# Three more blocks of the next layer's rows made ahead of a layer's last turn (graph layers, one core)

## Chip, cores and metric

One core of a Trainium2 chip (trn2). The metric is the device time of one execution in microseconds, the median of several runs. The profile is one execution on the chip, taken by the hardware profiler.

## What is computed

3125 nodes with 128 features, 103125 edges with one of 9 types. Three relational layers, then a residual and a layer norm, then an attention layer over the same edges with a second residual and norm. The change touches only the three relational layers:

```python
out = embeddings
for l in range(3):
    X = einsum('ne,ref->rnf', out, weights[l])          # 9 products for each node
    msg = X[edge_type, src] + biases[l][edge_type]      # one row for each edge
    hidden = segment_sum(msg, dest, num_segments=3125)  # added up by destination
    out = relu(hidden) if l + 1 < 3 else hidden
```

## The kernel before

**Rows of a layer.** The nodes are cut into 25 blocks of 128. For a block, TensorE multiplies the block (in `hB`) with the layer's nine weight matrices in three matmul groups (`make_x`, L1176), VectorE adds the bias and puts the three results into one of five slots of `xst` (`take_made`, L676, one add for each group, called a make below), and SyncE stores the slot to the layer's table in HBM (`store`, L901, one DMA of 576 KB).

**Tiles and steps.** The edges are sorted by destination and cut into 806 tiles of 128 edges. GpSimd gathers the 128 rows of a tile from the table with one indirect DMA (L1010) into one of 62 slots of `grow`. SyncE waits for each tile in order and passes it on (L907). The destinations are cut into 31 groups of 102 nodes. A layer is 840 steps in 35 turns of 24: a step multiplies a tile with a one-hot matrix of one group (TensorE L1132; VectorE makes the one-hot at L581 and adds the product to the group's sums `hn` at L652). A tile that crosses a group's border is used in two steps. Where a tile is used is data; by the end of a layer the step number runs some 30 ahead of the tile number. In the same turns 10 cells of a table of edge counts are multiplied (VectorE L586 and L587, five matmuls a cell at L1141), until all 840 cells are done, in turn 13 of the third layer. When a group's cells are complete, ScalarE copies and stores them (L1312 to L1325).

**Between layers.** A layer's table must be whole before the next layer's first gather, since any edge may point at any node. The sums of finished groups are turned (`turn_sums`, L1165), passed through relu to `hB` (`take_turned`, L662), and made into rows. Four early portions do this inside the layer: `AT_TURN` = turns 9, 16, 23 and 31 each begin with a portion of five blocks, on two PSUM banks (`PAIR_BANKS`). A portion stands in the program order of TensorE and VectorE ahead of its turn; it begins when all steps before it have been added, and the turn's steps come after it. SyncE issues the stores of a portion among the tiles it passes on (`STORE_AT`). After the layer's last step the late part follows on three banks: 6 groups are turned and blocks 20 to 24 made and stored. Then the again part turns the other 25 groups and makes blocks 0 to 19 a second time, whatever the data; its stores are conditional. They are done only where the edges were spread so unevenly that a portion ran before its groups were finished (`overrun`, `again_made`), which is tested once, when the groups' ends are known. Then the steps of the next layer begin.

**What GpSimd waits for.** Before the first gather of a layer it waits until the stores of all 25 blocks have landed (one semaphore for each slot of `xst`). After that a gather may not overwrite a slot that is in use: from tile 60 on, every fourth gather waits for a count of used steps (`s_used`): tile t waits until step t - 29 has been used. The first 60 gathers of a layer wait for nothing.

Of the kernel before, what the change touches and what calls it, by code (L numbers as in the profile page):

```python
# [22 lines left out]
I32 = mybir.dt.int32  # L23
I16 = mybir.dt.int16
ALU = mybir.AluOpType
# [3 lines left out]
P = 128  # L29
U = 8  # L30
HALF = 4
RB = 102
# [15 lines left out]
def gnn_program(nc, x, src, dst, edge_type, weights, biases, beta, out):  # L48
    N, D = x.shape
    E = src.shape[0]  # L50
    L, R = weights.shape[0], weights.shape[1]
    NB = -(-N // P)
# [14 lines left out]
    GT = -(-E // P)  # L67
# [31 lines left out]
    XU = 5  # L99
# [3 lines left out]
    XN = NB // XU  # L103
# [1 line left out]
    assert BANKS == 7  # L105
    WIDTH = [min(512, NP - 512 * c) for c in range(BANKS)]

    EARLY = NB // XU - 1
    BLOCKS = [range(XU * k, XU * k + XU) for k in range(EARLY)]
    LATE_BLOCKS = range(XU * EARLY, NB)  # L110
    REACH = [P * XU * (k + 1) // RB + 1 if P * XU * (k + 1) % RB else P * XU * (k + 1) // RB for k in range(EARLY)]
    GROUPS = [range(REACH[k - 1] if k else 0, REACH[k]) for k in range(EARLY)]
    CUT = P * XU * EARLY // RB
    LATE_GROUPS, AGAIN_GROUPS = range(CUT, MB), range(0, CUT)
    AGAIN_BLOCKS = range(0, XU * EARLY)
    AT_TURN = [-(-(REACH[k] * NT // MB + BODY) // BODY) for k in range(EARLY)]
    PAIR_BANKS, ALL_BANKS = (6, 7), (5, 6, 7)
    EARLY_STORES, ALL_STORES = EARLY + 1, 2 * EARLY + 1
    assert AT_TURN[-1] < TURNS and all(a < b for a, b in zip(AT_TURN, AT_TURN[1:]))
    STORE_AT = {}  # L120
    for k in range(EARLY):
        for j, b in enumerate(BLOCKS[k]):
            STORE_AT[AT_TURN[k] * BODY + 12 + 2 * j] = b
    assert len(STORE_AT) == len(AGAIN_BLOCKS) and max(STORE_AT) < GT

    CG = NB // JB
    CW = JB * RB
# [32 lines left out]
    with ExitStack() as ctx:  # L160
        def sb(name, shape, dt=F32):
            return ctx.enter_context(nc.sbuf_tensor(name, shape, dt))
# [33 lines left out]
        top = sb("top", [P, NB])  # L196
        rden = sb("rden", [P, NB])
        overrun = sb("overrun", [P, EARLY + 1])
        again_made = sb("again_made", [P, 2], I32)


        REGION = 26900
# [96 lines left out]
        s_xd = [sem(f"s_xd{u}") for u in range(XU)]  # L299
# [41 lines left out]
        def values_of(eng, a, k, most, n, least=0):  # L341

            return nc.values_load_multi_w_load_instructions(
                a[0:1, bass.ds(k * n, n)], engines=[eng.engine], min_val=least, max_val=most)[1]
# [22 lines left out]
        def reg_wait(eng, s, value):  # L367

            eng.wait_ge(s, value)
            eng.nop(nofuse=True)  # L370
# [3 lines left out]
        def _(dve):  # L374
# [15 lines left out]
            nc_ = dve  # L390
# [98 lines left out]
            for k in range(EARLY):  # L489
                ins = nc_.tensor_scalar(overrun[:, k:k + 1], te[:, REACH[k] - 1:REACH[k]], float(AT_TURN[k] * BODY), None, ALU.is_gt)  # L490
            step(ins)
            step(nc_.tensor_reduce(overrun[:, EARLY:EARLY + 1], overrun[:, 0:EARLY], AX.X, ALU.max))
            nc_.tensor_copy(again_made[:, 0:1], overrun[:, EARLY:EARLY + 1])
            nc_.tensor_scalar(again_made[:, 1:2], overrun[:, EARLY:EARLY + 1], float(16 * EARLY), None, ALU.mult)
            step(nc_.memset(ends[:, MB - 1:MB], CQ + 1), "ends")
            past_t = gix[:, 0:NT].bitcast(F32)
            step(nc_.tensor_scalar(past_t, iota_s, endcol[:, 0:1], None, ALU.is_ge), "past")
# [56 lines left out]
            for t in range(EP):  # L554
                k = t % KR
# [129 lines left out]
            for l in range(L):  # L685
                if l:
                    take_turned(LATE_GROUPS, ALL_BANKS)
                    take_made(l, LATE_BLOCKS, ALL_BANKS)
                    take_turned(AGAIN_GROUPS, ALL_BANKS)
# [3 lines left out]
                for i in range(0, TURNS):  # L693
                    if l < L - 1 and i in AT_TURN:
                        k = AT_TURN.index(i)
                        take_turned(GROUPS[k], PAIR_BANKS)
                        take_made(l + 1, BLOCKS[k], PAIR_BANKS)
                    take_tiles(l, i, i < full)
# [12 lines left out]
            for b in range(0, NB, 4):  # L711
                n = min(4, NB - b)
# [150 lines left out]
        def _(sp):  # L863
# [22 lines left out]
            for q in range(NB * XC):  # L886
                b, c = q // XC, q % XC
# [10 lines left out]
            def store(l, b, cond=None):  # L898
                given[0] += XC
                sp.wait_ge(s_xe, given[0])  # L900
                sp.dma_start(xv[l][b * P:(b + 1) * P, :, :],  # L901
                             xst[:, b % XU, :].rearrange("p (r d) -> p r d", r=R), cond=cond).then_inc(s_xd[b % XU], 16)

            def pass_on(l):
                for t in range(GT):
                    sp.wait_ge(s_g[t % GR], 16 * (ROUNDS * l + t // GR + 1))
                    sp.sem_inc(s_seq, 1)  # L907
                    if l < L - 1 and t in STORE_AT:
                        store(l + 1, STORE_AT[t])

            sp.wait_ge(s_d, marks["ends"])
            needed = values_of(sp, again_made, 0, 1, 1)[0]
            pass_on(0)
            for l in range(1, L):
                for b in LATE_BLOCKS:
                    store(l, b)
# [2 lines left out]
                pass_on(l)  # L919

            for u in range(XU):
                sp.wait_ge(s_xd[u], 16 * ALL_STORES * (L - 1))
            sp.wait_ge(s_cst, 32 * CG * MB)

            def load_absent(k):
# [26 lines left out]
            for i in range(XN):  # L952
                sp.wait_ge(s_res, i + 1)
                lo, hi = i * XU, min((i + 1) * XU, NB - 1)
# [6 lines left out]
        @block.gpsimd  # L961
        def _(pool):
            nc_ = pool
            nc_.memset(ident[:, :], 0.0).then_inc(s_pool, 1)
            nc_.memset(ltri, 1.0).then_inc(s_pool, 1)
            nc_.memset(ones[:, :], 1.0).then_inc(s_pool, 1)
            nc_.memset(diag[:, :], 0.0).then_inc(s_pool, 1)
            nc_.iota(iota_w[:, :], pattern=[[1, RB]], base=0, channel_multiplier=0,
                     allow_small_or_imprecise_dtypes=True).then_inc(s_pool, 1)
            nc_.iota(iota_s, pattern=[[1, NT]], base=0, channel_multiplier=0,  # L970
                     allow_small_or_imprecise_dtypes=True).then_inc(s_pool, 1)
            nc_.iota(steps_down[:, :].rearrange("p (b m) -> p b m", m=P), pattern=[[P, CG], [0, P]], base=0, channel_multiplier=1,
                     allow_small_or_imprecise_dtypes=True).then_inc(s_pool, 1)
            nc_.iota(number[:, :], pattern=[[P, TC]], base=0, channel_multiplier=1,
                     allow_small_or_imprecise_dtypes=True).then_inc(s_pool, 1)
            pool.wait_ge(s_pool, 8)
            nc_.affine_select(out=ident[:, :], in_=ident[:, :], compare_op=ALU.not_equal, fill=1.0, base=0,
                              pattern=[[-1, P]], channel_multiplier=1).then_inc(s_pool, 1)

            nc_.affine_select(out=ltri, in_=ltri, compare_op=ALU.is_gt, fill=0.0, base=0,  # L980
                              pattern=[[1, P]], channel_multiplier=-1).then_inc(s_pool, 1)
            pool.wait_ge(s_pool, 10)

            nc_.tensor_scalar(negi[:, :], ident[:, :], -1.0, None, ALU.mult).then_inc(s_pool, 1)
            nc_.tensor_copy(diag[:, P:2 * P], ident[:, :]).then_inc(s_pool, 1)
            pool.wait_ge(s_pool, 12)
            pool.sem_inc(s_pool, 1)

            pool.wait_ge(s_fill, 16)
            pool.wait_ge(s_d, marks["cells"])  # L990
            for t in range(CP):
                pool.indirect_dma_start(  # L992
                    out=table, out_offset=bass.IndirectOffsetOnAxis(ap=pay[:, t, 1:2], axis=0),
                    in_=pay[:, t, 0:1], in_offset=None).then_inc(s_scat, 16)

            pool.wait_ge(s_d, marks["rows"])
            again = values_of(pool, again_made, 1, 16 * EARLY, 1)[0]
            for l in range(L):
                if l == 0:
                    for u in range(X0):  # L1000
                        pool.wait_ge(s_x0d[u], 16 * (-(-(NB * XC - u) // X0)))
                else:
                    for u in range(XU):
                        reg_wait(pool, s_xd[u], again + 16 * (ALL_STORES * (l - 1) + EARLY_STORES))

                for t in range(GT):
                    last = t + SLOTS - 1 - GR + LAP
                    if t % SLOTS == 0 and t + SLOTS - 1 >= GR:
                        pool.wait_ge(s_used, NT // SLOTS * l + last // SLOTS + 1)
                    pool.indirect_dma_start(  # L1010
                        out=grow[:, t % GR * D:(t % GR + 1) * D], out_offset=None, in_=xts[l],
                        in_offset=bass.IndirectOffsetOnAxis(ap=gix[:, t:t + 1], axis=0),
                    ).then_inc(s_g[t % GR], 16)
# [3 lines left out]
        def _(pe):  # L1017
# [163 lines left out]
            for l in range(L):  # L1181
                if l:
                    turn_sums(LATE_GROUPS, ALL_BANKS, NT * l)
                    make_x(l, LATE_BLOCKS, ALL_BANKS)
                    turn_sums(AGAIN_GROUPS, ALL_BANKS, NT * l)
# [4 lines left out]
                for i in range(0, TURNS):  # L1190
                    if l < L - 1 and i in AT_TURN:
                        k = AT_TURN.index(i)
                        turn_sums(GROUPS[k], PAIR_BANKS, NT * l + i * BODY)
                        make_x(l + 1, BLOCKS[k], PAIR_BANKS)
                        pe.wait_ge(s_xe, made[0])
# [188 lines left out]
```

## Time and profile before

| what | value |
|---|---|
| median of 3 runs | 4012.15 us (4010.5 to 4013.2) |
| the profiled execution | 4012.3 us, its span 4010.6 us |
| TensorE (matmul) busy | 2913.1 us, 73% of the span |
| VectorE busy | 2799.0 us, 70% |
| GpSimd busy | 2586.7 us, 64% |
| ScalarE busy | 820.7 us, 20% |
| gathers from the tables of layers 1 and 2 | 1612, mean 945 ns |

A busy share is an average over stages with different limits. The stage that the change touches is short: the end of the first and of the second layer, and the first turns after it. It is read from the timeline there and from what each engine waited for. Times in rows count from the span's start; what stands in brackets at a row's end is the engine's idle time before it and what ended it.

### The profile page before, as it was taken

The numbers are of one execution on the slowest core, as the hardware profiler recorded it, in microseconds if no ns is written. First come the engines' busy times: TensorE is split into PE (matmuls) and PEld (weight loads), VectorE is DVE, ScalarE is ACT, GpSimd is POOL, SyncE is SP. The second block draws the span as 40 slices with busy tenths as digits, with TensorE's granted clock in tenths as the row PEclk, the third lists the DMA queues.
The fourth block names the chain that finished last, engine by engine and source line by source line (L and its number), as shares of the span: only waits on it lengthen the run. The fifth ranks groups of instructions, "written<-read, shape, count | busy, mean of one in ns | idle before, by whom it ended". The sixth has DMA issues, their size and how long they took to land.

```text
span 4010.6 us, 57296 instructions
## 1 busy us (share of the span) xinstructions
PE 2913.1 (73%) x14367; PEld 1879.1 (47%) x14369; DVE 2799.0 (70%) x9282; ACT 820.7 (20%) x1995; POOL 2586.7 (64%) x2738
## 2 busy tenths in 40 slices
PE   7799967677777678777777776787674444447998
PEld 4455544444444445444444443554443333335776
DVE  9988876676667667776767665878664333337999
ACT  2588810100110010100100010001100000004665
POOL 0677757777777775777777777567777777770000
PEclk9899988888889889998889888999885555557999
DMA  4100013443444343343344434333333221223664
GB/s 157 54 2 2 2 36 73 82 110 76 102 89 107 73 102 88 74 90 102 79 107 83 102 81 85 103 81 78 86 79 73 53 54 53 53 53 116 191 189 136
DMA packets 373882, 336.44 MB, mean 84 GB/s; under 512 B 262034, under 2 KB 326090, under 8 KB 373448
## 3 DMA queue, kind: packets, MB, share of 16 engines
q0 software_dynamic: 87104, 158.80, 18.8%
q1 hardware_dynamic: 83112, 113.25, 8.5%
q10 hardware_dynamic: 203360, 60.73, 6.3%
q8 instruction: 141, 2.31, 0.2%
q14 instruction: 165, 1.35, 0.1%
HBM read 225.44 MB, written 130.73 MB: 89 GB/s over the span
## 4 chain that ended last, share of the span: by engine, by line
POOL 43%; PE 24%; issue 16%; DVE 12%; DMA 3%; ACT 2%; DVEq 0%; SPq 0%; POOLq 0%; ACTq 0%
POOL region L1010 43%; PE ps L1087 9%; PE ps L1132 4%; PE ps L1141 3%; PE ps L1215 3%; DMA region<-x_of_type_in_layer,arrays 2%; PE ps L1243 2%; DVE region L652 2%; PE ps L1176 2%; DVE region L586 1%; DVE region L419 1%; DVE region L587 1%; DVE region L779 1%; DVE arrays L453 1%; DVE arrays L464 1%
## 5 line engine op out<-in xcount | busy, mean ns | idle before, releaser
L1010 POOL DMA_INDIRECT region<-x_of_type_in_layer,arrays x1612 | 1522.7, 945 | 552.0 <-issue 475.1
L1132 PE MATMUL ps<-region,oh 128*102 x5040 | 1115.0, 325 | 781.7 <-SPq L907 514.8
L1132 PEld LDWEIGHTS ps<-region,oh 128*102 128x102 f32 x5040 | 922.3, 204 | 1337.1 <-issue 1078.0
L1141 PE MATMUL ps<-region 128*128 128x510 f16 x4200 | 1358.8, 411 | 180.2 <-ACT ps L1301 136.2
L581 DVE TENSOR_SCALAR oh<-iota_w,arrays 128x102 f32<-128x102 f32 x2528 | 727.0, 289 | 1046.5 <-PE ps L1132 1022.7
L1010 POOL DMA_INDIRECT region<-x_of_type,arrays x806 | 763.7, 947 | 273.2 <-issue 272.0
L652 DVE TENSOR_TENSOR region<-region,ps 102x128 f32 x2520 | 714.9, 284 | 3.9 <-issue 3.9
L1141 PEld LDWEIGHTS ps<-region 128*128 128x128 f16 x4200 | 434.6, 104 | 247.6 <-issue 195.1
L1312 ACT COPY region<-ps 128x510 f32<-128x510 f32 x155 | 89.8, 579 | 2244.7 <-PE ps L1141 2244.2
L586 DVE TENSOR_SCALAR region<-ps,arrays 128x640 f16<-128x640 f16 x844 | 460.1, 545 | 0.0
L992 POOL DMA_INDIRECT scattered_edges<-region x304 | 296.2, 974 | 208.7 <-DVE shiftcol L483 110.4
L587 DVE TENSOR_SCALAR region<-ps,arrays 128x510 f16<-128x510 f16 x844 | 400.5, 475 | 0.0
L1087 PE MATMUL ps<-region 128*128 128x420 f16 x2016 | 362.4, 341 | 23.7 <-ACT region L1282 23.7
L1282 ACT ACTIVATE region<-region 128x128 f16<-128x128 f16 x1008 | 310.3, 389 | 71.0 <-DVE region L559 70.7
L1087 PEld LDWEIGHTS ps<-region 128*128 128x128 f16 x2016 | 195.8, 97 | 190.7 <-ACT region L1282 24.8
L560 DVE TENSOR_SCALAR region<-region 128x840 f16<-128x840 f16 x504 | 262.0, 520 | 0.0
L1176 PE MATMUL ps<-wsb,hB 128*128 128x384 f32 x540 | 212.4, 548 | 8.8 <-DVE hB L662 8.4
L676 DVE TENSOR_TENSOR region<-ps,bias 128x384 f32<-128x384 f32 x270 | 148.9, 552 | 66.4 <-PE ps L1176 63.0
L1243 PEld LDWEIGHTS ps<-nodes,region 128*128 128x128 f32 (+1 forms) x1250 | 163.9, 191 | 53.8 <-DVE region L779 28.5
L1243 PE MATMUL ps<-nodes,region 128*128 128x129 f32 (+1 forms) x1250 | 181.3, 282 | 7.2 <-DVE region L779 7.0
L1215 PE MATMUL ps<-hB,region 128*128 128x384 f32 (+1 forms) x450 | 170.9, 461 | 0.0
L1176 PEld LDWEIGHTS ps<-wsb,hB 128*128 128x128 f32 x540 | 104.8, 208 | 112.0 <-DVE region L676 53.0
(222 smaller groups left out, 1671.7 us busy)
## 6 DMA issues: line engine op xcount, KB each, us to landing
x_of_type_in_layer<-region SPq DMA_DIRECT2D x90, 576.0 KB
edge_counts<-region ACTq DMA_DIRECT2D x155, 255.0 KB
arrays<-edge_counts SPq DMA_DIRECT2D x40, 960.0 KB, 5.1
region<-x_of_type_in_layer,arrays POOLq DMA_INDIRECT x1612, 2.6
edge_absent<-region ACTq DMA_DIRECT2D x155, 127.5 KB
region<-edge_absent SPq DMA_DIRECT2D x40, 480.0 KB, 4.3
region<-x_of_type,arrays POOLq DMA_INDIRECT x806, 2.6
x_of_type<-x0st SPq DMA_DIRECT2D x51, 192.0 KB, 1.8
```

Source lines behind the costliest of these rows:

```text
L581: ins = nc_.tensor_scalar(oh[:, t % U, 0:RB], iota_r, rowf[:, t % NT:t % NT + 1], None, ALU.is_equal)
L586: nc_.tensor_scalar(cl[:, q % CR, :], lane_h, key1[:, q:q + 1], None, ALU.is_equal)
L587: nc_.tensor_scalar(cr[:, q % CR, :], lane_h[:, 0:CW], key2[:, q:q + 1], None, ALU.is_equal).then_inc(s_co, 1)
L652: nc_.tensor_tensor(h, h, ps[0:RB, 6 + n % 2, t * D:(t + 1) * D], ALU.add).then_inc(s_add, 1)
L992: pool.indirect_dma_start(out=table, out_offset=bass.IndirectOffsetOnAxis(ap=pay[:, t, 1:2], axis=0), in_=pay[:, t, 0:1], in_offset=None). ...
L1010: pool.indirect_dma_start(out=grow[:, t % GR * D:(t % GR + 1) * D], out_offset=None, in_=xts[l], in_offset=bass.IndirectOffsetOnAxis(ap=gi ...
L1087: mm = pe.matmul(ps[:, 2 * d + n, 0:HW], oh_q[:, k, d, :], oh_s[:, k, n * HW:(n + 1) * HW], start=False, stop=False, skip_group_check=True)
L1132: mm = pe.matmul(ps[0:RB, 6 + n % 2, t * D:(t + 1) * D], oh[:, u % U, 0:RB], grow[:, bass.ds(at[u % PAIRS], D)], start=True, stop=True)
L1141: mm = pe.matmul(ps[:, c, 0:CW], cl[:, q % CR, c * P:(c + 1) * P], cr[:, q % CR, :], start=False, stop=False, skip_group_check=True)
L1176: pe.matmul(ps[:, banks[j % len(banks)], 0:G3], hB[:, b * P:(b + 1) * P], wsb[:, l * R + 3 * c:l * R + 3 * c + 3, :].rearrange("p r d -> p ...
L1243: mm = pe.matmul(ps[0:w, 4 + c % 2, t * VW:(t + 1) * VW], ring[:, b % RING, t * P:t * P + w], nodes[:, j, :], start=False, stop=(j == NB - ...
L1282: ins = act.activation(oh_q[:, k, d, :], hot_q[:, k, :], ACT.Copy, scale=cols[:, 4 * t + 2 + d:4 * t + 3 + d])
```

## The change

The list of portions is now given by the blocks at which they end: 5, 10, 15, 20 and 23. A fifth portion, with blocks 20, 21 and 22 (nine makes) and three groups to turn (26 to 28), stands ahead of turn 34, the last of a layer. The late part turns three groups (28 to 30) and makes blocks 23 and 24; the again part turns 28 groups and makes 23 blocks. The stores of blocks 20 to 22 would fall after tile 805, so SyncE issues them once all tiles of the layer are passed on. Since blocks 23 and 24 use slots 3 and 4, the slots now have different numbers of conditional stores, and GpSimd reads two numbers for its waits instead of one. The test of the groups' ends covers the fifth portion too, with one more compare.

```diff
-    EARLY = NB // XU - 1
-    BLOCKS = [range(XU * k, XU * k + XU) for k in range(EARLY)]
-    LATE_BLOCKS = range(XU * EARLY, NB)
-    REACH = [P * XU * (k + 1) // RB + 1 if P * XU * (k + 1) % RB else P * XU * (k + 1) // RB for k in range(EARLY)]
+    ENDS_AT = list(range(XU, NB, XU)) + [NB - 2]
+    EARLY = len(ENDS_AT)
+    BLOCKS = [range(lo, hi) for lo, hi in zip([0] + ENDS_AT, ENDS_AT)]
+    LATE_BLOCKS = range(ENDS_AT[-1], NB)
+    REACH = [-(-P * b // RB) for b in ENDS_AT]
     GROUPS = [range(REACH[k - 1] if k else 0, REACH[k]) for k in range(EARLY)]
-    CUT = P * XU * EARLY // RB
+    CUT = P * ENDS_AT[-1] // RB
     LATE_GROUPS, AGAIN_GROUPS = range(CUT, MB), range(0, CUT)
-    AGAIN_BLOCKS = range(0, XU * EARLY)
+    AGAIN_BLOCKS = range(0, ENDS_AT[-1])
     AT_TURN = [-(-(REACH[k] * NT // MB + BODY) // BODY) for k in range(EARLY)]
-    EARLY_STORES, ALL_STORES = EARLY + 1, 2 * EARLY + 1
+    FIRST_STORES = XN
+    AGAIN_STORES = [sum(b % XU == u for b in AGAIN_BLOCKS) for u in range(XU)]
...
+            nc_.tensor_scalar(again_made[:, 1:2], overrun[:, EARLY:EARLY + 1], float(16 * (XN - 1)), None, ALU.mult)
+            nc_.tensor_scalar(again_made[:, 2:3], overrun[:, EARLY:EARLY + 1], float(16 * XN), None, ALU.mult)
...
                     if l < L - 1 and t in STORE_AT:
                         store(l + 1, STORE_AT[t])
+                for t in sorted(STORE_AT) if l < L - 1 else ():
+                    if t >= GT:
+                        store(l + 1, STORE_AT[t])
...
-            again = values_of(pool, again_made, 1, 16 * EARLY, 1)[0]
+            again = [values_of(pool, again_made, n, 16 * XN, 1)[0] for n in (1, 2)]
...
-                        reg_wait(pool, s_xd[u], again + 16 * (ALL_STORES * (l - 1) + EARLY_STORES))
+                        reg_wait(pool, s_xd[u], again[AGAIN_STORES[u] - XN + 1] + 16 * (FIRST_STORES * l + AGAIN_STORES[u] * (l - 1)))
```

## Rows read from the trace of the kernel before

**Rows 1.** What GpSimd waited for: total us, times, longest us.

```profile
POOL region L1010 <- DMA x_of_type_in_layer<-region: 58.3, 2, 29.4
POOL region L1010 <- PE ps L1132: 19.8, 55, 2.4
```

**Rows 2.** Timeline of GpSimd: start us, us, what, [idle before, what ended it].

```profile
1575.74 0.94 POOL L1010 DMA_INDIRECT region<-x_of_type_in_layer,arrays  x1 [28.90 <-DMA x_of_type_in_layer<-region]
...
1652.79 0.94 POOL L1010 DMA_INDIRECT region<-x_of_type_in_layer,arrays  x1 [2.40 <-PE ps L1132]
...
2613.85 0.94 POOL L1010 DMA_INDIRECT region<-x_of_type_in_layer,arrays  x1 [29.43 <-DMA x_of_type_in_layer<-region]
...
2689.70 0.94 POOL L1010 DMA_INDIRECT region<-x_of_type_in_layer,arrays  x1 [1.24 <-PE ps L1132]
```

**Rows 3.** Busy us (instructions): stretch, length, PE, PEld, DVE, ACT, POOL, PEclk, DMA, GB/s.

```profile
1575.74:1652.79 77.05, 65.55 (x256) 39.62 (x256) 56.91 (x160) 8.11 (x13) 56.66 (x60) 0.93 0.28 69
```

**Rows 4.** Timeline of VectorE at the end of layer 0: last add, makes.

```profile
1556.91 0.29 DVE L652 TENSOR_TENSOR region<-region,ps 102x128 f32 x1
...
1560.86 0.56 DVE L676 TENSOR_TENSOR region<-ps,bias 128x384 f32<-128x384 f32 x1 [1.81 <-PE ps L1176]
...
1566.50 1.78 DVE L676 TENSOR_TENSOR region<-ps,bias 128x384 f32<-128x384 f32 x3 [0.16 <-PE ps L1176]
...
1570.37 1.78 DVE L676 TENSOR_TENSOR region<-ps,bias 128x384 f32<-128x384 f32 x3 [0.16 <-PE ps L1176]
```

**Rows 5.** Timeline of VectorE, two blocks of the again part after layer 0.

```profile
1577.15 1.13 DVE L676 TENSOR_TENSOR region<-ps,bias 128x384 f32<-128x384 f32 x2 [1.07 <-PE ps L1176]
...
1579.09 1.13 DVE L676 TENSOR_TENSOR region<-ps,bias 128x384 f32<-128x384 f32 x2 [0.16 <-PE ps L1176]
```

**Rows 6.** Timeline of VectorE, layer 0: fourth portion and turn 31 after it.

```profile
1444.34 0.29 DVE L652 TENSOR_TENSOR region<-region,ps 102x128 f32 x1
...
1448.45 0.56 DVE L676 TENSOR_TENSOR region<-ps,bias 128x384 f32<-128x384 f32 x1 [1.81 <-PE ps L1176]
...
1455.88 0.56 DVE L676 TENSOR_TENSOR region<-ps,bias 128x384 f32<-128x384 f32 x1 [0.15 <-PE ps L1176]
...
1460.65 0.56 DVE L676 TENSOR_TENSOR region<-ps,bias 128x384 f32<-128x384 f32 x1 [0.16 <-PE ps L1176]
...
1468.82 0.28 DVE L652 TENSOR_TENSOR region<-region,ps 102x128 f32 x1
...
1486.62 0.29 DVE L652 TENSOR_TENSOR region<-region,ps 102x128 f32 x1
```

**Rows 7.** Busy us and granted clock, TensorE in two stretches of that portion.

```profile
1446.60:1451.50 4.90, 4.80 (x8) 2.42 (x8) 1.72 (x4) 0.00 (x0) 3.68 (x5) 0.50 0.53 86
1451.50:1461.30 9.80, 9.01 (x24) 3.42 (x22) 6.70 (x12) 0.00 (x0) 7.36 (x9) 1.00 0.43 79
```

**Rows 8.** Timeline of VectorE, the adds around the dearest and cheapest portion.

```profile
1010.22 0.29 DVE L652 TENSOR_TENSOR region<-region,ps 102x128 f32 x1
...
1035.88 0.28 DVE L652 TENSOR_TENSOR region<-region,ps 102x128 f32 x1
...
2048.03 0.29 DVE L652 TENSOR_TENSOR region<-region,ps 102x128 f32 x1
...
2071.35 0.28 DVE L652 TENSOR_TENSOR region<-region,ps 102x128 f32 x1
```

**Rows 9.** Timeline of VectorE: last adds of turns 33 and 34.

```profile
1534.21 0.29 DVE L652 TENSOR_TENSOR region<-region,ps 102x128 f32 x1
...
2575.13 0.29 DVE L652 TENSOR_TENSOR region<-region,ps 102x128 f32 x1
...
2595.79 0.29 DVE L652 TENSOR_TENSOR region<-region,ps 102x128 f32 x1
```

**Rows 10.** Timeline of ScalarE, layer 2: the 29th of 31 groups of counts.

```profile
2889.40 2.42 ACT L1318 ACTIVATE region<-region,big 128x2550 bf16<-128x2550 f32 x1
```

**Rows 11.** Busy us (instructions) of the cells' matmuls (L1141) after that.

```profile
2889.40:3100.00 210.60, 83.37 (x245) 26.38 (x245) 0.74 0.39 81
```

More of the change, by code:

```diff
@@ L106, in gnn_program @@
     WIDTH = [min(512, NP - 512 * c) for c in range(BANKS)]
-    EARLY = NB // XU - 1
-    BLOCKS = [range(XU * k, XU * k + XU) for k in range(EARLY)]
-    LATE_BLOCKS = range(XU * EARLY, NB)
-    REACH = [P * XU * (k + 1) // RB + 1 if P * XU * (k + 1) % RB else P * XU * (k + 1) // RB for k in range(EARLY)]
+    ENDS_AT = list(range(XU, NB, XU)) + [NB - 2]
[3 more added lines that the diff above has]
+    REACH = [-(-P * b // RB) for b in ENDS_AT]
     GROUPS = [range(REACH[k - 1] if k else 0, REACH[k]) for k in range(EARLY)]
-    CUT = P * XU * EARLY // RB
+    CUT = P * ENDS_AT[-1] // RB
     LATE_GROUPS, AGAIN_GROUPS = range(CUT, MB), range(0, CUT)
-    AGAIN_BLOCKS = range(0, XU * EARLY)
+    AGAIN_BLOCKS = range(0, ENDS_AT[-1])
     AT_TURN = [-(-(REACH[k] * NT // MB + BODY) // BODY) for k in range(EARLY)]
     PAIR_BANKS, ALL_BANKS = (6, 7), (5, 6, 7)
-    EARLY_STORES, ALL_STORES = EARLY + 1, 2 * EARLY + 1
+    FIRST_STORES = XN
+    AGAIN_STORES = [sum(b % XU == u for b in AGAIN_BLOCKS) for u in range(XU)]
+    assert NB == XU * XN and set(AGAIN_STORES) <= {XN - 1, XN}
     assert AT_TURN[-1] < TURNS and all(a < b for a, b in zip(AT_TURN, AT_TURN[1:]))
@@ L123, in gnn_program @@
             STORE_AT[AT_TURN[k] * BODY + 12 + 2 * j] = b
-    assert len(STORE_AT) == len(AGAIN_BLOCKS) and max(STORE_AT) < GT
+    assert sorted(STORE_AT.values()) == list(AGAIN_BLOCKS)
     CG = NB // JB
@@ L198, in gnn_program @@
         overrun = sb("overrun", [P, EARLY + 1])
-        again_made = sb("again_made", [P, 2], I32)
+        again_made = sb("again_made", [P, 3], I32)
         REGION = 26900
@@ L493, in _ @@
             nc_.tensor_copy(again_made[:, 0:1], overrun[:, EARLY:EARLY + 1])
-            nc_.tensor_scalar(again_made[:, 1:2], overrun[:, EARLY:EARLY + 1], float(16 * EARLY), None, ALU.mult)
+            nc_.tensor_scalar(again_made[:, 1:2], overrun[:, EARLY:EARLY + 1], float(16 * (XN - 1)), None, ALU.mult)
+            nc_.tensor_scalar(again_made[:, 2:3], overrun[:, EARLY:EARLY + 1], float(16 * XN), None, ALU.mult)
             step(nc_.memset(ends[:, MB - 1:MB], CQ + 1), "ends")
@@ L921, in _ @@
             for u in range(XU):
-                sp.wait_ge(s_xd[u], 16 * ALL_STORES * (L - 1))
+                sp.wait_ge(s_xd[u], 16 * (FIRST_STORES + AGAIN_STORES[u]) * (L - 1))
             sp.wait_ge(s_cst, 32 * CG * MB)
```

## Prediction

> **What bounds the kernel now.** I read the waits of GpSimd first, then its timeline at the two layer borders, then what VectorE and TensorE do around them. In the waits, the gathers of layers 1 and 2 lose 58.3 us to two waits for the stored rows, one at each border, and 19.8 us in 55 pieces to TensorE [rows 1]. The timeline says where: GpSimd stands still for 28.90 and 29.43 us before the first gather of layers 1 and 2 [rows 2]. That gap is what the change shortens. The next row of the same timeline matters more: after 60 gathers that wait for nothing [rows 3], the gather of tile 60 is held by TensorE for 2.40 us in layer 1 and 1.24 us in layer 2 [rows 2]. The 60 gathers take 75 us, and the hold lasts until step 31 of the new layer has been used. So at both borders two chains run side by side: GpSimd's (stores, then 60 gathers) and the consumer's, meaning TensorE and VectorE (late part, again part, 32 steps). The consumer's is the longer one, by about 2 and 1 us. From tile 60 on GpSimd sets the pace, so the time at which tile 60 goes out carries through to the layer's end. What moves the total is the moment at which step 31 is used, not the moment of the first gather.
>
> **The late part gets shorter.** At full clock a block costs 1.935 us there (from 1566.50 to 1570.37 for two blocks [rows 4]); three blocks less are 5.8 us. Turning three groups less saves a little: from the last add to the first make it is 3.66 us with six groups (1557.20 to 1560.86 [rows 4]) and 3.82 us with seven (1444.63 to 1448.45 [rows 6]), so 0.16 us a group and 0.5 us for three. Stores leave as each block is made, so the last one leaves 6.3 us sooner after the last add.
>
> **The again part gets longer by the same.** It makes three blocks and turns three groups more. A block costs 1.94 us (1577.15 to 1579.09 [rows 5]): +5.8 and +0.5 us. From a layer's last add to its successor's step 31 the consumer has the same work as before, since late and again part together always make 25 blocks. For it the change at the border is 0.
>
> **The fifth portion is new work.** It isn't moved work: its three blocks are made again behind the border. Its nearest row is the fourth portion in layer 0. There VectorE's last add ends at 1444.63 and its next one begins at 1468.82: 24.19 us without a step [rows 6]. Of this, 3.82 us pass before the first make, 12.76 us are 15 makes, and 7.61 us pass from the last make (ends 1461.21) to the next add. The new portion has nine makes: makes 10 to 15 took 4.77 us (from the end of the ninth, 1456.44, to 1461.21). It has four groups less to turn: 0.6 us. That leaves 24.19 - 4.77 - 0.64 = 18.8 us. The eight portions of before lie between 23.03 us (2048.32 to 2071.35) and 25.37 us (1010.51 to 1035.88) [rows 8], which gives 17.6 to 20.0 us.
>
> The restart is part of this price: TensorE ran at half its clock (0.50, 1.2 GHz) for the first 4.9 us of the fourth portion's makes, 8 matmuls in 4.80 us, and at 1.00 (2.4 GHz) for the next 24 in 9.01 us [rows 7]. The Trainium skill, TensorE: Matmul & The Clock Gate, Part 1, says that the throttled state is the default and activity releases it, which speaks against cutting work into one more portion. By a portion that began at full clock the price would be about 1.8 us less (8 matmuls at 0.375 instead of 0.60 us); the trace shows the half clock, and the sum keeps it.
>
> **What hides it.** Only waiting that the consumer already does in turn 34. After a portion tiles are plentiful and 24 steps run at VectorE's own pace: 18.1 us from first add to last (1468.82 to 1486.91 [rows 6]). I take this for the new turn 34; all its tiles will have landed by then, since GpSimd's last gather goes out 28.9 us before 1575.74 [rows 2]. So from the last add of turn 33 to the last add of the layer: 18.8 + 18.1 = 36.9 us. Before it was 1534.50 to 1557.20 = 22.7 us in layer 0 (with [rows 4]) and 2575.42 to 2596.08 = 20.7 us in layer 1 [rows 9]. The layer's last add moves by +14.2 and +16.2 us.
>
> **Sum.** GpSimd's first gather moves by 14.2 - 6.3 = +7.9 us at the first border and by 16.2 - 6.3 = +9.9 us at the second, against its own earlier pace: even the gap that was to shrink grows, to about 36.8 and 39.3 us. Tile 60 waits for the consumer and moves by +14.2 and +16.2 us, so its hold grows by 6.3 us each, to about 8.7 and 7.5 us. Both shifts reach the end, since GpSimd paces layer 1 after tile 60 and all of layer 2: 14.2 + 16.2 = 30.4 us. On the profiled execution's 4012.3 us (span 4010.6) that is 4042.7; the median of the runs is 0.15 us lower, so 4042.5 us.
>
> **Edits taken as nothing.** One more compare and one more product on single columns of VectorE in the setup: an add of 102x128 takes 0.29 us [rows 4], so at most 0.6 us; below nothing it can't be. One register load more on GpSimd lies ahead of the first gathers, where it waits anyway, and is under the same bound. SyncE: the three stores come behind the last tile it passes on, so no tile waits behind them; by then their makes are done (portion from 1534.50, 3.2 us and 8.0 us of makes, so about 1546), and they land long before the two late stores. If that cover failed, a store would be late by no more than the two behind it, some 4 us of GpSimd's chain, which has 6.3 us of slack against the consumer's. The portion's slots 0 to 2 of xst hold blocks whose stores went out among tiles 756 to 760, some 30 tiles before the portion.
>
> **Rivals.** (a) *The portion costs nothing.* If the consumer waited for tiles in turn 34 for the portion's whole length, only the border would count: the first gather comes 6.3 us earlier, and tile 60 is held 6.3 us longer. 4012, no change. For it: TensorE does wait for tiles over much of the program. Against it: the slack in turn 34 is 22.7 and 20.7 us less 18.1, under 5 and 3 us, against 18.8.
>
> (b) *The gain that the change reaches for, faster.* Hidden portion, and tile 60 not held: GpSimd is the pace, and it starts 6.3 us earlier twice, 4012.15 - 12.6 = 3999.6. It decides if GpSimd's chain is the longer one; the rows show the hold by TensorE at both borders before the change [rows 2], so it needs two things to be wrong at once. The busy times over those 77 us can't decide it: VectorE 56.91, GpSimd 56.66 us [rows 3]. The Trainium skill, Perfetto Trace Analysis, Optimization Strategy, has one look for the gaps of the most-contended engine and make what they wait for come sooner; with GpSimd taken for it, that rule leads to this rival, and the 2.40 and 1.24 us holds behind the gap are what it would overlook.
>
> (c) *The portion costs what I say, but tile 60 isn't held.* Only GpSimd's start counts: 7.9 + 9.9 = 17.8 us, 4030. It needs the consumer to be some 6 us faster behind the border than before; nothing in the rows offers that.
>
> (d) *Dearer.* A group's counts come to be copied within turn 34 or the hold grows into later tiles: a few us at each border, 4050 or more.
>
> (e) *It doesn't do what it says.* If group 28 ended after step 816, where turn 34 begins, all blocks would be stored a second time and GpSimd would wait for 23 blocks of 1.94 us at each border, some 45 us on top of the shift of its first gather (7.9 and 9.9 us), about 4120. The counts of the 29th group are complete at 2889.40 [rows 10], and 245 matmuls, five a cell, come after [rows 11]: it ends at cell 840 - 49 = 791, below 816. Excluded but for an error of mine.
>
> **How the numbers follow.** Forecast 0.78, (a) 0.06, (b) 0.04, (c) 0.07, (d) 0.04, (e) 0.01. The forecast's own range: portions of 17.6 to 20.0 us give 28.0 to 32.8 us, and with 1 us a border for the turn's pace and the small edits 4039 to 4047. To hold 8 in 10 the range reaches to (c) and the near part of (d): 4029 to 4050. A measurement of this kernel tells 0.2% (8 us) from no change: slower 0.78 + 0.07 + 0.04 + 0.01 = 0.90, same 0.06, faster 0.04.
>
> **What would show it.** Right: between the last add of turn 33 and the first of turn 34 some 19 us without a step in layers 0 and 1; GpSimd's gaps at the borders near 37 and 39 us; tile 60 held for about 8 us; layer 2 shifted as a whole by 30 us. Wrong: an unchanged last add (the portion is hidden), tile 60 not held (GpSimd sets the border), or a second pass of stores that lengthens the gap to 70 us or more.

## The result

| | kernel before | changed kernel |
|---|---|---|
| median, measured side by side (6 runs each) | 4012.56 us | 4040.49 us |
| profiled execution, its span | 4012.3 us, 4010.6 us | 4039.88 us, 4038.1 us |
| ratio, 95% interval | | 1.0071 (1.0058 to 1.0083) |

The changed kernel is slower by 28 us, 0.7%; forecast were 4042.5 us and slower. Nearly all of it is at the two layer borders. First GpSimd's timeline in the changed kernel, the rows that answer to [rows 2] (start us, us, what, idle before and what ended it):

```profile
1580.40 0.94 POOL L1017 DMA_INDIRECT region<-x_of_type_in_layer,arrays  x1 [33.10 <-DMA x_of_type_in_layer<-region]
...
1663.47 0.94 POOL L1017 DMA_INDIRECT region<-x_of_type_in_layer,arrays  x1 [8.44 <-PE ps L1139]
...
2636.23 0.94 POOL L1017 DMA_INDIRECT region<-x_of_type_in_layer,arrays  x1 [41.34 <-DMA x_of_type_in_layer<-region]
...
2717.15 0.94 POOL L1017 DMA_INDIRECT region<-x_of_type_in_layer,arrays  x1 [6.31 <-PE ps L1139]
```

The gap that the change was to shorten has grown at both borders, from 28.90 and 29.43 to 33.10 and 41.34 us. The hold of tile 60 has grown too, from 2.40 and 1.24 to 8.44 and 6.31 us. Tile 60 goes out 10.7 us later in layer 1 (1652.79 to 1663.47) and 27.5 us later in layer 2 (2689.70 to 2717.15). After that nothing is added: the spans differ by 27.5 us. In total, by the waits of GpSimd (us, times, longest), against [rows 1]:

```profile
POOL region L1017 <- DMA x_of_type_in_layer<-region: 74.4, 2, 41.3
POOL region L1017 <- PE ps L1139: 30.6, 54, 8.4
```

16.1 us more for the stored rows and 10.8 us more for TensorE make 26.9 of the 27.5 us. The cause stands ahead of the border, in VectorE's timeline around the fifth portion in layer 0 (last add before it, first and last make, first add after it) and then at the layer's end, answering to [rows 6] and [rows 4]:

```profile
1532.36 0.29 DVE L656 TENSOR_TENSOR region<-region,ps 102x128 f32 x1
...
1535.52 0.56 DVE L680 TENSOR_TENSOR region<-ps,bias 128x384 f32<-128x384 f32 x1 [1.81 <-PE ps L1183]
...
1542.44 0.56 DVE L680 TENSOR_TENSOR region<-ps,bias 128x384 f32<-128x384 f32 x1 [0.36 <-PE ps L1183]
...
1549.41 0.28 DVE L656 TENSOR_TENSOR region<-region,ps 102x128 f32 x1
...
1567.83 0.29 DVE L656 TENSOR_TENSOR region<-region,ps 102x128 f32 x1
...
1575.03 1.78 DVE L680 TENSOR_TENSOR region<-ps,bias 128x384 f32<-128x384 f32 x3 [0.71 <-PE ps L1183]
```

From 1532.65 to 1549.41 no step is added: 16.8 us. The layer's last add ends at 1568.12 instead of 1557.20. The late part then ends at 1576.81, and the first gather comes 12.3 us after the last add (1568.12 to 1580.40) where it came 18.5 us after it before (1557.20 to 1575.74). So the late part did get 6.3 us shorter, as the change intends. At the second border 17.8 us became 10.8 (2596.08 to 2613.85 before, 2625.39 to 2636.23 now).

In layer 1 the portion was longer:

```profile
2584.99 0.29 DVE L656 TENSOR_TENSOR region<-region,ps 102x128 f32 x1
...
2607.30 0.28 DVE L656 TENSOR_TENSOR region<-region,ps 102x128 f32 x1
...
2625.10 0.29 DVE L656 TENSOR_TENSOR region<-region,ps 102x128 f32 x1
```

22.0 us without a step (2585.28 to 2607.30), and the last add at 2625.39 instead of 2596.08: 29.3 us later, of which 10.7 were brought along from the first border.

### The profile page after: what moved, and what is told of

Same layout as the page of the kernel before. It is cut to its first block, busy times and chain, and to the rows that moved or that the text cites. A ratio compares the mean times of both kernels' runs of the same rounds, so it can differ in the third digit from the quotient of the medians.

```text
span 4038.1 us, 57436 instructions
## 1 busy us (share of the span) xinstructions
PE 2917.9 (72%) x14411; PEld 1879.9 (47%) x14411; DVE 2808.1 (70%) x9308; ACT 819.7 (20%) x1995; POOL 2585.2 (64%) x2738
## 4 chain that ended last, share of the span: by engine, by line
POOL 42%; PE 25%; issue 16%; DVE 12%; DMA 3%; ACT 2%; DVEq 0%; SPq 0%; POOLq 0%; ACTq 0%
POOL region L1017 42%; PE ps L1094 9%; PE ps L1139 4%; PE ps L1148 4%; PE ps L1222 3%; DMA region<-x_of_type_in_layer,arrays 2%; PE ps L1183 2%; PE ps L1250 2%; DVE region L656 2%; DVE region L590 2%; DVE region L422 1%; DVE region L591 1%; DVE region L783 1%; DVE arrays L456 1%; DVE arrays L467 1%
## 5 line engine op out<-in xcount | busy, mean ns | idle before, releaser
L1183 PE MATMUL ps<-wsb,hB 128*128 128x384 f32 x576 | 229.6, 552 | 10.5 <-DVE hB L666 9.5
L680 DVE TENSOR_TENSOR region<-ps,bias 128x384 f32<-128x384 f32 x288 | 159.6, 555 | 75.2 <-PE ps L1183 72.6
```

What stands on the lines that cost most here:

```text
L1183: pe.matmul(ps[:, banks[j % len(banks)], 0:G3], hB[:, b * P:(b + 1) * P], wsb[:, l * R + 3 * c:l * R + 3 * c + 3, :].rearrange("p r d -> p ...
```

## Experiments

Each run was timed beside the kernel before on the same chip; its ratio is to that kernel there. The medians of before beside them were 4015.35 us (the first four) and 4014.57 us (the last four), so times are compared by their difference to before. The changed kernel's is 28 us. Rows of two runs differ by a few us without a cause in the edit: up to the end of turn 33 of layer 0 the kernels of e1, e3 and e8 do the same as the kernel before, and that turn ended between 1532.0 and 1537.5 us in their traces (1534.5 in that of before).

| run | us above before | ratio (95% interval) |
|---|---|---|
| e1, before without the again part | -1.0 | 0.9998 (0.9989 to 1.0007) |
| e2, changed without the again part | 18.9 | 1.0049 (1.0035 to 1.0062) |
| e3, portion added, its rows unused | 27.0 | 1.0067 (1.0054 to 1.0081) |
| e5, a portion of one block | 23.1 | 1.0058 (1.0045 to 1.0072) |
| e6, early stores later | 26.0 | 1.0071 (1.0057 to 1.0085) |
| e7, changed, register loads first | 7.9 | 1.0020 (1.0011 to 1.0029) |
| e8, empty portion | 10.7 | 1.0030 (1.0019 to 1.0040) |
| e9, before, register loads first | -2.3 | 0.9995 (0.9986 to 1.0004) |

**Is the shorter late part worth anything?** e3 keeps the whole late part and adds the portion as dead work. In the kernel before:

```diff
+                    if l < L - 1 and i == TURNS - 1:
+                        turn_sums(range(26, 29), PAIR_BANKS, NT * l + i * BODY)
+                        make_x(l + 1, range(20, 23), PAIR_BANKS)
+                        pe.wait_ge(s_xe, made[0])
                     use_tiles(l, i, i < full)
```

(VectorE takes the sums and the makes likewise; SyncE stores nothing of it.)

> The kernel before with the fifth portion added as pure extra work: three groups turned and nine makes ahead of turn 34, nothing stored, and the late part makes all five blocks as before. Theory (what the late part saves is lost again in the hold of tile 60): the same time as the changed kernel, 4040.5 (4038 to 4043), with a longer gap at the borders (about 39 and 46 us instead of 33 and 41) and a short hold of tile 60 (about 2 and 1 us instead of 8 and 6). Rival (what counts is GpSimd's gap, and the change did win 6.3 us a border in the late part): 12.6 us above the changed kernel, 4053.

27.0 us above before, the same as the changed kernel within the intervals, and not 12.6 us dearer. Its GpSimd rows:

```profile
1590.95 0.94 POOL L1014 DMA_INDIRECT region<-x_of_type_in_layer,arrays  x1 [43.78 <-DMA x_of_type_in_layer<-region]
...
1668.22 0.94 POOL L1014 DMA_INDIRECT region<-x_of_type_in_layer,arrays  x1 [2.66 <-PE ps L1136]
...
2648.65 0.94 POOL L1014 DMA_INDIRECT region<-x_of_type_in_layer,arrays  x1 [48.56 <-DMA x_of_type_in_layer<-region]
```

The gaps are 10.7 and 7.2 us longer than in the changed kernel: from the last add to the first gather it took 18.5 and 20.0 us instead of 12.3 and 10.8. The hold of tile 60 in layer 1 is back at 2.66 us; in layer 2 there is none. What the late part saves in the gap is lost in the hold. The saving of 6.3 us a border is real in the gap and not to be seen in the time. At the second border the two chains are close: in e3 step 31 was used 93.3 us after the last add and tile 60 went out 94.9 us after it (2628.68 to 2723.57), so there GpSimd's chain was the longer one by about 1.3 us, and so much of the saving may count; the times don't resolve that. The Trainium skill, Perfetto Trace Analysis, Optimization Strategy, looks for the gaps of the engine one optimizes and makes what they wait for come sooner; here that moved a gap's end without moving the end of the next wait, 75 us behind it.

**Is it the consumer's chain?** e1 and e2 take the again part out of both kernels (and with it what provides for uneven edges; the sums are cleared by one instruction instead). TensorE's part; VectorE, SyncE and GpSimd drop theirs likewise:

```diff
                     make_x(l, LATE_BLOCKS, ALL_BANKS)
-                    turn_sums(AGAIN_GROUPS, ALL_BANKS, NT * l)
-                    make_x(l, AGAIN_BLOCKS, ALL_BANKS)
```

> The kernel before without the again part (the second making of blocks 0 to 19 at each border and its conditional stores; one clearing of the sums takes its place), so what is left out is the provision for uneven edges. Theory (the border has two chains, and the consumer's, TensorE and VectorE, is the longer one by 2.1 and 0.9 us before the change): tile 60 is no longer held, the first gathers stay where they are (gaps about 29 us), and the total falls by about 3 us: 4009.5, between 4008 and 4011. Rival (the again part's 44 us a border are themselves on the path): 20 us or more are gained, 3990 or less.

> The changed kernel without the again part, as in the run beside it. Theory: with the consumer's chain shortened only GpSimd's chain is left, so the fifth portion costs what it moves the first gathers, 4.7 and about 11.7 us as the changed kernel's trace shows them: 16 us above the kernel before without the again part, about 4026 (4023 to 4029), tile 60 not held. Rival (the portion costs its 28 us wherever the border's limit is): 4037 or more. Rival (without the again part the shorter late part pays): 4009 or less.

In e1 the gaps stayed (28.77 and 28.55 us) and no wait for TensorE exceeded 0.3 us, which is the pace's own. The time fell by 1.0 us, less than the 3 expected, with an interval that holds both. The trace is of an execution of 4005.9 us, 8.5 us below e1's median, so its rows show that the holds went, and not how much time that saved. That the again part is on the path with its 44 us is refuted. e2's rows:

```profile
1584.51 0.94 POOL L1014 DMA_INDIRECT region<-x_of_type_in_layer,arrays  x1 [36.52 <-DMA x_of_type_in_layer<-region]
...
2634.61 0.94 POOL L1014 DMA_INDIRECT region<-x_of_type_in_layer,arrays  x1 [43.41 <-DMA x_of_type_in_layer<-region]
```

```profile
POOL region L1014 <- PE ps L1136: 17.4, 57, 0.3
```

No hold is left, only the longer gaps. The portion now costs 19.9 us (e2 against e1) instead of 28: some 8 us are given back where the holds of before and after differ by 11 (8.44 + 6.31 less 2.40 + 1.24). It is 4 us more than the 16 expected, with portions of 19.0 and 21.7 us where the changed kernel had 16.8 and 22.0. The shorter late part does pay here (from the last add to the first gather 9.4 and 11.1 us, in e1 18.5 and 17.2), but the later last add costs more.

**What of the price is the stop, what the makes?** e8 puts an empty portion into the kernel before (as e3, with `range(0)` for its blocks); e5 is the changed kernel with one block in the portion:

```diff
-    ENDS_AT = list(range(XU, NB, XU)) + [NB - 2]
+    ENDS_AT = list(range(XU, NB, XU)) + [NB - 4]
```

> The kernel before with an empty fifth portion ahead of turn 34: three groups are turned and nothing is made. It measures what the stop alone costs. Theory: 9.3 us in layer 0 and 12 us in layer 1 (the unused portion of nine makes, 16.8 and 20.1 us, less its makes, 7.6 and 8.1 us), of which turn 34 hides 4 and 2 us: 15 us above the kernel before (12 to 19), more than half of the changed kernel's 28. Rival (the price is the nine makes): within 4 us of the kernel before.

> The changed kernel with a fifth portion of one block (one group turned, three makes, by the program's own rule ahead of turn 32), four blocks left at the end. Theory (most of a portion's price is the stop itself): a portion of about 14 us, of which turns 32 to 34 hide some 5 us in layer 0 and 2 us in layer 1: 22 us above the kernel before, about 4034 (4028 to 4037). Rival (the price goes with the makes): a third of the 28 us, about 4022. Rival (a smaller and earlier portion is hidden): 4012.

The empty portion, layer 0, VectorE from the last add before it to the first add after it:

```profile
1531.70 0.29 DVE L652 TENSOR_TENSOR region<-region,ps 102x128 f32 x1
1532.57 0.48 DVE L662 TENSOR_SCALAR hB<-ps 128x306 f32<-128x306 f32 x1 [0.57 <-PE ps L1169]
...
1541.50 0.28 DVE L652 TENSOR_TENSOR region<-region,ps 102x128 f32 x1
```

9.5 us without a step (1531.99 to 1541.50) for 0.48 us of VectorE's work; 10.5 us in layer 1. By its length the stop is about half of a portion of nine makes (16.8 and 22.0 us in the changed kernel, 16.8 and 20.1 us in e3): the pipeline runs dry, is filled with a few turned sums, and is started again. By the time it is less than half: 10.7 us of the 28, below the 12 to 19 expected. Turn 34 hid 4.3 and 2.6 us of the two stops, as assumed. But the second stop was 1.5 us shorter than expected, and in this trace turn 33 of layer 0 ended 2.5 us earlier than in that of before (1531.99 against 1534.50), so that tile 60 of layer 1 went out only 2.7 us later (1652.79 to 1655.52). That the price is the nine makes alone is refuted.

One block cost 23.1 us as expected, with portions of 17.3 us in layer 0 and 13.3 us in layer 1; a price by makes (9 us) is refuted. A portion of three makes costs some five sixths of one of nine. It doesn't follow how the price grows from none to three makes: e5's portion turns one group instead of three and stands ahead of turn 32, with two more turns behind it, and in layer 0 its two register loads, which are told of next, took 1.98 and 2.24 us beside stores of the fourth portion.

**What makes layer 1's portion longer?** The way from the last make to the first use of a tile took 2.7 us in layer 0 and 5.2 us in layer 1. TensorE has two register loads there: it reads numbers that the program has worked out, such as the slots of the tiles to use, into its registers (`steps_at`, L357, and `banks_at`, L365). The loads of `banks_at` (duration ns min/median/max): behind the portion in layer 1, in layer 0, and over the second half of the turns with cells:

```profile
L365 PEldq TENSOR_LOAD <-region x1: 3272/3272/3272, 2597.9 to 2597.9; - x1
```

```profile
L365 PEldq TENSOR_LOAD <-arrays x1: 1071/1071/1071, 1544.2 to 1544.2; - x1
```

```profile
L365 PEldq TENSOR_LOAD <-region x42: 1070/1078/3272, 1795.1 to 3021.8; - x42
```

In layer 1 the three early stores had just left, at 2596.7 to 2597.6 us; in layer 0 they left at 1549.1, behind the loads (GpSimd's last gather was earlier against the portion in layer 1). In e2's layer 1 the other load met them, begun as the third store left:

```profile
L357 PEldq TENSOR_LOAD <-x0st x1: 3452/3452/3452, 2593.9 to 2593.9; - x1
```

e6 holds the stores back:

```diff
                     if t >= GT:
+                        sp.wait_ge(s_used, NT // SLOTS * l + (TURNS - 1) * BODY // SLOTS + 5)
                         store(l + 1, STORE_AT[t])
```

> The changed kernel with its three early stores held until TensorE has used steps 832 to 835 of the layer. In the changed kernel TensorE's register load after the fifth portion took 3.27 us in layer 1, with the three stores in flight, and 1.07 us in layer 0, where they left later. Theory (the stores slow that load): both loads of the restart take about 1.08 us in both layers, layer 1's portion falls from 22.0 to about 20 us, and the total is 2 to 3 us below the changed kernel, about 25 us above the kernel before (24 to 27). Rival (the load is long for another reason): it stays at 3 us and the time stays at 28 us above.

```profile
L365 PEldq TENSOR_LOAD <-region x1: 1072/1072/1072, 2597.7 to 2597.7; - x1
```

The load is back at 1.07 us and layer 1's portion at 20.0 us, so the stores did slow it. What that is worth in time is not shown. The 26.0 us lie in the expected 24 to 27, but their interval doesn't tell them from the changed kernel's 28, and the two spans are alike (4037.7 and 4038.1 us). In layer 1 the last add came 1.9 us earlier (2623.52 against 2625.39), and from there to the use of step 31 it took 1.7 us more (93.2 against 91.5). In layer 0, whose stores left after its loads in both kernels, the portion was 20.0 us instead of 16.8, and the way from the last add to step 31 was 90.8 us instead of 95.1, so that tile 60 went out at 1662.98, no later than in the changed kernel (1663.47).

These differences go with TensorE's clock. In the portion of layer 0 it is 2.4 of the 3.3 us at the restart: from the first use of a tile to the first add 6.08 us at a mean of 0.50, instead of 3.70 us at 1.00. From that layer's last add to the next layer's first add it was granted 1.00, in the changed kernel 0.92. In the changed kernel both cases stand side by side (busy us (instructions) of PE, PEld, DVE, ACT, POOL, then the granted clock; layer 0, layer 1):

```profile
1545.70:1549.40 3.70, 3.69 (x23) 2.69 (x24) 1.03 (x3) 0.00 (x0) 1.30 (x2) 1.00 0.14 39
2601.70:2607.30 5.60, 5.54 (x23) 3.67 (x24) 1.04 (x3) 0.00 (x0) 0.00 (x0) 0.66 0.03 13
```

The same 23 matmuls, 3.69 us at 1.00 (2.4 GHz) and 5.54 us at a mean of 0.66, part of the stretch at 1.2 GHz. TensorE had been idle for 3.3 us before the first and 5.8 us before the second. Which case a portion gets changes from run to run for the same instructions: 3.70 us in layer 0 of e3, 6.08 us in e2 and e6.

**Can the restart be made cheaper?** e7 and e9 issue the register loads of a portion's turn and of a layer's first turn ahead of the portion and of the late part, where TensorE waits for the last adds anyway:

```diff
-                        at, due = steps_at((i * BODY + u) // PAIRS)
+                        at, due = loaded[0] if loaded and u == 0 else steps_at((i * BODY + u) // PAIRS)
...
                         k = AT_TURN.index(i)
+                        loaded = loads(l, i, i < full)
                         turn_sums(GROUPS[k], PAIR_BANKS, NT * l + i * BODY)
...
```

> The changed kernel with TensorE's register loads of a portion's turn, and of a layer's first turn, issued ahead of the portion or of the late part instead of behind it, where TensorE waits for VectorE's last adds anyway. Theory (the consumer's chain sets both borders, tile 60 being held 8 and 6 us, so what it is spared comes back in full): 2.2 us less at the restart in layer 0, 4.5 us less in layer 1, and 2.2 us less at the start of layers 1 and 2, some 11 us below the changed kernel, 14 to 20 us above the kernel before. Rival (GpSimd's gap at the border sets the time): only what the last add gains counts, some 6 us below the changed kernel. Rival (the loads are hidden already): no difference.

> The kernel before with the same earlier register loads. Theory (its consumer's chain is only 2.1 and 0.9 us longer than GpSimd's): the 2.2 us that it is spared at each border remove the hold of tile 60 and no more, 3 us below the kernel before, up to 5 where the fourth portion's shorter restart also brings the last add forward. Rival (the consumer's chain is the longer one by far): 4 to 5 us at each border, 9 us below. Rival (GpSimd's gap alone counts): no difference in the gaps and none in the time.

e7 is 7.9 us above before, 20 us below the changed kernel, where 11 were expected. TensorE in layer 0 behind the portion: 1.05 us idle, and the first uses at full pace.

```profile
1542.25 0.46 PE L1142 MATMUL ps<-region,oh 128*102 x2 [1.05 <-DVE region L680]
1542.55 0.81 PE L1151 MATMUL ps<-region 128*128 128x510 f16 x3
1543.19 0.38 PE L1142 MATMUL ps<-region,oh 128*102 x2
```

The fifth portions were 14.3 and 15.6 us. What I had not counted is the clock and the other portions: after the short idle time the first add came 3.70 to 3.76 us behind the first use in the fourth and fifth portions of both layers, and the fourth portions fell from 23.0 and 24.4 to 19.9 and 20.7 us, so turn 33 ended sooner too. The clock in the fifth portions, from the first use on, in layers 0 and 1:

```profile
1542.25:1545.95 3.70, 3.70 (x23) 2.69 (x24) 1.04 (x3) 0.00 (x0) 2.83 (x3) 1.00 0.19 53
2586.59:2590.29 3.70, 3.70 (x23) 2.70 (x24) 1.04 (x4) 0.00 (x0) 0.98 (x2) 1.00 0.14 35
```

It was at 1.00 on that way in all 18 portions of e7 and e9, behind 1.0 to 1.2 us of idle time. In the other eight kernels' 76 portions, behind 3.2 to 6.1 us, that was so in nine. That the shorter idle time keeps the clock up is the likely reading; no run changes it without the loads. In the profiled executions 17.3 us were saved. 7.2 of them were there at tile 60 of layer 1 (1663.47 to 1656.27): 1.0 by an earlier turn 33, 2.5 in the portion, 0.6 in turn 34 and 3.1 between the last add and step 31. The rest came in layer 1 and at its border. Both rivals, 6 us and none, are refuted; the theory had the direction, and half of the size.

e9 is 2.3 us below before (3 were expected), which its interval doesn't tell from no change. From the last add to the use of step 31 it took 90.0 and 90.9 us instead of 95.3 and 93.4. No wait of GpSimd for TensorE exceeded 0.3 us, and the gaps were 27.63 and 29.34 us: the hold was all that it could remove. With the loads first in both kernels, the fifth portion costs 10.2 us (e7 against e9) instead of 28.

## Why the prediction was right

- **What bounds the border: right.** Tile 60 was held for 8.4 and 6.3 us (forecast about 8.7 and 7.5), and its shift went through to the end. e3 shows it by itself: with and without the saving in the late part the time is the same. e2 shows the other side: with the consumer's chain short the holds vanish, and the portion costs less.
- **Late part 6.3 us shorter: right.** From last add to first gather 18.5 us became 12.3 us, and 17.8 us became 10.8 us at the second border.
- **Late and again part together the same: right.** From last add to the use of step 31 it took 95.3 us before and 95.1 us after at the first border, 93.4 and 91.5 us at the second. Of the 1.9 us there, 1.7 are the clock: from the new layer's first use of a tile to its first add 5.38 us before (granted 0.68) and 3.70 us after (1.00).
- **Portion 18.8 us, between 17.6 and 20.0: right in the mean, wrong in the bounds.** 16.8 and 22.0 us, mean 19.4: one portion below the bounds and one above, so that the mean fits is in part luck. The bounds came from the eight portions of before, by their sums only. The three parts of a restart vary on their own: the register loads (1.07 us each, 3.27 with stores in flight), the half clock at the first makes, which was in the sum, and the half clock at the first uses (3.70 to 6.08 us), which was not set apart.
- **Last add later by 14.2 and 16.2 us: off by 3 and 2 us, in opposite ways.** It was 10.9 and 18.6 us. In layer 0 turn 33 also ended 1.85 us earlier (1532.65 against 1534.50), 1.2 us of it by the fourth portion, which took 23.0 us this time instead of 24.2. In layer 1 the portion was 3.2 us longer than forecast and turn 33 ended 0.8 us earlier against the first border. The full-pace turn 34 was as assumed, 18.7 and 18.1 us against 18.1.
- **First gather later by 7.9 and 9.9 us:** 4.7 and 11.7 us, for the same reason.
- **Sum 30.4 us:** 27.5 us in the profiled executions, 27.9 us in the medians. Two errors of opposite sign cancel; that the sum came out within 3 us owes something to that.
- **SyncE's stores taken as nothing: wrong in its reason, small in its size.** No tile waited behind them, as forecast, but they slowed a register load of TensorE by 2.2 us in layer 1. The forecast looked for waits between them, and no wait joins them; where a store and a register load meet is not shown, nor what it cost in time.

## What to carry to other kernels

Ahead of shortening a gap, look for the next wait of the same engine behind it: if that one is ended by another chain, the gap's gain only lengthens it. A portion of other work cut into a running pipeline costs the stop and the restart, here 9.5 to 10.5 us a time without any makes, and this must be set against what it moves. Where such a stop is kept, issue the restart's register loads ahead of it: here the portion's price fell from 28 to 10 us when both kernels did so.

## What the runs showed of the hardware

- A register load on TensorE's queue took 1.07 to 1.08 us where nothing disturbed it (median of 42 in the changed kernel: 1078 ns), 3.27 us there and 3.45 us in e2 where three stores of 576 KB had just left, and 1.07 us with the stores moved away.
- Where TensorE restarted after 3.3 and 5.8 us of idle time, the same 23 matmuls took 3.69 and 5.54 us, by its granted clock (1.00 and a mean of 0.66). Behind 3.3 us both cases were seen, 3.70 us in the changed kernel and 6.08 us in e6 to the first add. After 1.0 to 1.2 us of idle time they were at full pace in all 18 portions of e7 and e9.
